# Layer 2's expert blocks: stages two blocks apart with four places between them, and the key numbers loaded ahead of SyncE's fills

## The reference

```
x = hidden_states.reshape(-1, 256)
routing_weights = softmax(x @ gate)                       # 32 experts
top_k_weights, top_k_indices = top_k(routing_weights, 4)
top_k_weights = top_k_weights / top_k_weights.sum(-1)
g, u = split(x @ gate_up_proj[e], 2)                      # 2 x 96 columns
next_states = (u * silu(g)) @ down_proj[e]                # 96 -> 256
out = sum over the 4 chosen experts of weight * next_states
```

## Time and profile before

| | |
|---|---|
| median of 3 runs | 1046.31 us (1046.28 to 1047.95) |
| profiled execution, first to last instruction | 1040.2 us |
| TensorE (weight loads) busy | 862.0 us, 83% (674.7 us, 65%) |
| VectorE, ScalarE, GpSimd busy | 575.4, 359.2, 389.4 us |
| gate/up and down products of the blocks, L742 and L760 | 89.4 and 99.3 us, the latter with layer index 3's |
| scatters of the 95 blocks, L817 | 94.9 us, 999 ns each |
| chain of work that ended last | traced from the end back to 526 us |

### The profile page before, as it was taken

The page is one execution under the profiler, slowest core; times in us unless marked ns, Lnnn a source line. Parts: engine busy times, 40 slices in busy tenths (PEclk is TensorE's granted clock), DMA queues, the critical chain, the costliest instruction groups (busy, mean ns, idle before and its releaser), DMA issues.

```text
span 1040.2 us, 17487 instructions
## 1 busy us (share of the span) xinstructions
PE 862.0 (83%) x5237; PEld 674.7 (65%) x5237; DVE 575.4 (55%) x1679; ACT 359.2 (35%) x1007; POOL 389.4 (37%) x411
## 2 busy tenths in 40 slices
PE   2999998912789899777657898988995998999997
PEld 2787786601667677566546777868553675777786
DVE  5647886550556665628736887943352435444333
ACT  3425242420223333211236777821152323222221
POOL 7210725465345555657534554000046201343100
PEclk9999999965899999978858999995995999999999
DMA  9143205597454444176347776500242201332212
GB/s 352 33 168 75 83 22 185 202 247 191 104 175 131 124 125 142 48 243 226 95 109 163 171 164 154 139 1 1 91 127 82 89 11 58 103 97 83 86 56 107
DMA packets 67244, 126.49 MB, mean 122 GB/s; under 512 B 20004, under 2 KB 49085, under 8 KB 64515
## 3 DMA queue, kind: packets, MB, share of 16 engines
q1 hardware_dynamic: 45407, 74.42, 23.7%
q0 software_dynamic: 20960, 48.76, 16.3%
q10 hardware_dynamic: 788, 2.19, 0.9%
HBM read 87.39 MB, written 43.30 MB: 126 GB/s over the span
## 4 chain that ended last, share of the span: by engine, by line
PE 30%; DMA 8%; DVE 6%; issue 2%; ACT 2%; SPq 2%; POOL 0%; DVEq 0%; POOLq 0%; ACTq 0%
PE ps L460 9%; PE ps L742 5%; PE ps L760 3%; DMA big<-newblk,new_i 2%; PE ps L2396 2%; PE ps L2293 1%; PE ps L2441 1%; PE ps L2335 1%; DMA big<-big 1%; DMA early<-big 1%; DVE work L1861 1%; DVE early L1867 1%; SPq L995 1%; DMA big<-early 1%; PE ps L2397 1%
## 5 line engine op out<-in xcount | busy, mean ns | idle before, releaser
L826 POOL DMA_INDIRECT sent_d<-mid,slot_i x88 | 98.3, 1117 | 117.9 <-DVE mid L621 69.1
L817 POOL DMA_INDIRECT back_d<-early,mid x95 | 94.9, 999 | 90.5 <-DVE early L801 54.1
L760 PE MATMUL ps<-early 96*128 (+1 forms) x346 | 99.3, 387 | 0.7 <-DVE early L795 0.4
L771 ACT ACTIVATE early<-ps 128x256 f32<-128x256 f32 x134 | 51.4, 384 | 133.5 <-PE ps L732 100.7
L788 DVE TENSOR_TENSOR early<-early,ps 128x96 f32<-128x96 f32 (+1 forms) x134 | 37.2, 278 | 106.3 <-ACT early L776 65.9
L742 PE MATMUL ps<-big,early 128*128 x380 | 89.4, 359 | 6.9 <-ACT early L771 3.4
L494 DVE TENSOR_TENSOR hidl<-work,hidh 128x512 fp32r<-128x512 f32 (+1 forms) x56 | 38.7, 691 | 84.4 <-ACT hidh L487 83.7
L817 POOL DMA_INDIRECT back_d<-big,mid x39 | 38.4, 985 | 116.8 <-DVE big L801 114.4
L500 ACT ACTIVATE work<-ps 128x512 f32<-128x512 f32 (+1 forms) x56 | 33.4, 596 | 138.9 <-PE ps L460 136.9
L742 PEld LDWEIGHTS ps<-big,early 128*128 128x128 f32 x380 | 62.1, 197 | 20.9 <-issue 18.2
L732 PE MATMUL ps<-late,mid 128*128 128x128 f32 x268 | 53.2, 281 | 26.7 <-DMA mid<-sent_d,first_i 23.1
(11 more groups left out here) (399 smaller groups left out, 2102.3 us busy)
## 6 DMA issues: line engine op xcount, KB each, us to landing
mid<-sent_d SPq DMA_DIRECT2D x124, 130.0 KB
big<-back_d SPq DMA_DIRECT2D x16, 512.0 KB
early<-back_d SPq DMA_DIRECT2D x16, 256.0 KB, 3.0
early<-in_w SPq DMA_DIRECT2D x3, 1024.0 KB, 11.4
big<-in_gate SPq DMA_DIRECT2D x1, 3072.0 KB, 10.6
big<-in_up SPq DMA_DIRECT2D x1, 3072.0 KB, 15.9
early<-in_gu SPq DMA_DIRECT2D x1, 2816.0 KB, 10.2
sent_d<-work SPq DMA_DIRECT2D x19, 130.0 KB
```

The costliest lines, as they stand in the source:

```text
L760: last = nc.tensor.matmul(ps[:, 6 + j % 2, 0:D], L.hTb[j % 2][0:f1 - f0, h * P:(h + 1) * P], L.down[0:f1 - f0, h, bass.ds(owners[j] * D, D ...
L771: nc.scalar.activation(L.yTb[b % 2], ps[:, b % 2, 0:2 * P], ACT.Copy).then_inc(s["turn_sb"], 1)
L817: nc.gpsimd.indirect_dma_start(out=back_d, out_offset=bass.IndirectOffsetOnAxis(ap=xblk[b % XRING][:, D:D + 1].bitcast(I32), axis=0), in_= ...
L826: nc.gpsimd.indirect_dma_start(out=sent_d, out_offset=bass.IndirectOffsetOnAxis(ap=L.slot_i[:, i:i + 1], axis=0), in_=L.rows[c][:, t, n, : ...
```

## The change

`L1.lag` is 2 and `L3.lag` 1. In turn b TensorE takes T of block b, the gate/up product of block b - lag, the hidden transpose of block b - 2 lag, the down product of block b - 3 lag; ScalarE and VectorE follow. For layer index 1 the loops so have 3 more turns, `yTb`, `hb` and `hTb` have four places (LRING), `sgb`, `ob` and the PSUM banks what they had. Waits for a place to come free now ask for the block four earlier, those for a PSUM bank for the block two earlier, as before. The mask's scratch moves in `early`. On SyncE the wait for `rows_ps` and the load of the key numbers move ahead of the wait for the tables and the fills. Layer index 3 keeps distance 1 and two places.

```diff
+LRING = 4
+L1.lag, L3.lag = 2, 1
...
-        yTb, sgb, hb, hTb, ob = (ring(0, 2, 2 * P), ring(512, 2, F1), ring(704, 2, F1), ring(896, 2, P),
-                                 ring(1152, ORING, D))
+        yTb, sgb, hb, hTb, ob = (ring(0, LRING, 2 * P), ring(1024, 2, F1), ring(1216, LRING, F1), ring(1600, LRING, P),
+                                 ring(2112, ORING, D))
...
-            if 1 <= b <= NB:
-                j = b - 1
+            if lag <= b < NB + lag:
+                j = b - lag
...
-            if 2 <= b <= NB + 1:
-                j = b - 2
+            if 2 * lag <= b < NB + 2 * lag:
+                j = b - 2 * lag
...
-            if b >= 3:
-                j = b - 3
+            if b >= 3 * lag:
+                j = b - 3 * lag
...
+            lag, ring_y = L.lag, len(L.yTb)
             if b < L.NB:
                 act.wait_ge(s["turn_ps"], L.turn0 + b + 1)
-                if b >= 2:
-                    act.wait_ge(s["pair_ps"], L.b0 + b - 1)
-                nc.scalar.activation(L.yTb[b % 2], ps[:, b % 2, 0:2 * P], ACT.Copy).then_inc(s["turn_sb"], 1)
+                if b >= ring_y:
+                    act.wait_ge(s["pair_ps"], L.b0 + b - ring_y + 1)
+                nc.scalar.activation(L.yTb[b % ring_y], ps[:, b % 2, 0:2 * P], ACT.Copy).then_inc(s["turn_sb"], 1)
...
+            sp.wait_ge(s["rows_ps"], NT)
+            k0 = first_at["key"][0]
+            assert first_at["keyless"][0] == k0 + WK
+            sp.dma_start(zm[:, 0:2 * WK], a["first"][:, k0:k0 + 2 * WK]).then_inc(s["keys"], 16)
             sp.wait_ge(s["tables"], AT_FILLS)
             for e in FILLS[0]:
                 r = sp.value_load(L1.endrow_i[0:1, e:e + 1], min_val=e * SPAN1, max_val=e * SPAN1 + T)
                 sp.dma_start(*fill_rows(r, e)).then_inc(s["filled"], 16)
-            sp.wait_ge(s["rows_ps"], NT)
-            k0 = first_at["key"][0]
-            assert first_at["keyless"][0] == k0 + WK
-            sp.dma_start(zm[:, 0:2 * WK], a["first"][:, k0:k0 + 2 * WK]).then_inc(s["keys"], 16)
...
-            for b in range(NBK + 3):
+            for b in range(NBK + 3 * L1.lag):
                 pe_block(pe, L1, b, owners)
```

More of the change, by code:

```diff
@@ L721, in pe_block @@
         def pe_block(pe, L, b, owners):
-            F, NB = L.F, L.NB
+            F, NB, lag = L.F, L.NB, L.lag
             if b < NB:
@@ L751, in pe_block @@
                 for h, (f0, f1) in enumerate(L.parts):
-                    last = nc.tensor.transpose(ps[0:f1 - f0, 4 + j % 2, h * P:(h + 1) * P], L.hb[j % 2][:, f0:f1], ident)
+                    last = nc.tensor.transpose(ps[0:f1 - f0, 4 + j % 2, h * P:(h + 1) * P],
+                                               L.hb[j % len(L.hb)][:, f0:f1], ident)
                 last.then_inc(s["hturn_ps"], 1)
-            if b >= 3:
-                j = b - 3
+            if b >= 3 * lag:
+                j = b - 3 * lag
                 pe.wait_ge(s["hturn_sb"], L.b0 + j + 1)
@@ L759, in pe_block @@
                 for h, (f0, f1) in enumerate(L.parts):
-                    last = nc.tensor.matmul(ps[:, 6 + j % 2, 0:D], L.hTb[j % 2][0:f1 - f0, h * P:(h + 1) * P],
+                    last = nc.tensor.matmul(ps[:, 6 + j % 2, 0:D],
+                                            L.hTb[j % len(L.hTb)][0:f1 - f0, h * P:(h + 1) * P],
                                             L.down[0:f1 - f0, h, bass.ds(owners[j] * D, D)],
@@ L779, in dve_block @@
+            if b >= lag:
+                j = b - lag
+                act.wait_ge(s["pair_ps"], L.b0 + j + 1)
+                if j >= 2:
+                    act.wait_ge(s["prod_sb"], L.b0 + j - 1)
+                nc.scalar.activation(L.sgb[j % 2], ps[:, 2 + j % 2, 0:L.F], ACT.Silu).then_inc(s["act_ready"], 1)
         def dve_block(dve, L, b):
-            F, n = L.F, len(L.parts)
+            F, n, lag = L.F, len(L.parts), L.lag
+            ring_h, ring_t = len(L.hb), len(L.hTb)
             w = L.parts[0][1]
-            if 1 <= b <= L.NB:
-                j = b - 1
+            if lag <= b < L.NB + lag:
+                j = b - lag
@@ L1267, in _ @@
                 act.dma_start(*fill_rows(r, e)).then_inc(s["filled"], 16)
-            for b in range(NBK + 1):
+            for b in range(NBK + L1.lag):
                 act_block(act, L1, b)
@@ L1431, in _ @@
             split_rows(3)
-            for b in range(NB3 + 1):
+            for b in range(NB3 + L3.lag):
                 act_block(act, L3, b)
@@ L2041, in _ @@
             split_rest(3)
-            for b in range(NB3 + 3):
+            for b in range(NB3 + 3 * L3.lag):
                 dve_block(dve, L3, b)
@@ L2481, in _ @@
             owners = {}
-            for b in range(NB3 + 3):
-                if b == 3:
+            for b in range(NB3 + 3 * L3.lag):
+                if b == 3 * L3.lag:
                     pe.wait_ge(s["acc_used"], 3 * NCH + 2)
```

30 lines of the change are left out of this document (12 added, 18 removed).

## The result

The changed kernel took 1035.11 us (median of 4 runs, 1030.98 to 1040.15) against 1047.13 us for the kernel before on the same chip: 0.9868 of it, 95% interval 0.982 to 0.9916. It is faster by 12 us. I had forecast 28.8 us and 1017.5 us, with a range up to 1035.0.

A forecast was written before the change was run, and what follows sets the result against it. Layer 1's expert blocks bound it: a 9.31 us hole at the start, 28.1 us lost to late releases. 431.74 - 402.0 - 0.9 = 28.8 us gained; span 1040.2 - 28.8 = 1011.4, plus 6.1 around it, 1017.5 us; range 1008.5 to 1035.

The forecast's parts named there:

- Key numbers ahead of the fills: Start of layer 1's expert blocks: VectorE's wait for keys goes, block 10's transpose starts at 267.8 instead of 278.15, 10.4 us won.
- The clock: Sign in layer 1's first blocks: TensorE's granted clock at 1.00 by 258.
- Blocks 12 to 17: Loads behind layer 2's weights: stretch stays 11.1 us, longer hole before block 17, block 18 3.36 us later; 10.7 us won so far.
- Stages two blocks apart: Layer 1's loop, blocks 18 to 94: more slack per hand-over cuts 135.96 us to 116.9, 1.54 us a step.
- The floor: Layer 1's loop, blocks 18 to 94: TensorE needs 76 x 1.42 = 107.9 us.
- 28.1 us that I called lost: Same loop: time beyond TensorE's 107.9 us, put down to late releases of results; a third, 9 us, was to stay.
- my 116.9 us: Forecast time of the loop from block 18 to 94: 107.9 + 9 us.
- The slack that I worked out: Layer 1's loop, two blocks apart: 1.4 us for PSUM hand-overs, covering releases 1.0 to 1.4 us late.
- The first rival: Layer 1's loop: late releases are TensorE's true pace, 1.79 us a step is work; 1036.5 us, chance 0.12.
- The tail: After block 94's transpose: seven scatters unsent instead of four, end 11.1 us later instead of 10.2; cost 0.9 us.
- The other rivals: Clock low to block 10 (0.07, 1025 us); GpSimd held by mask steps (0.05, 1024); scatters back late (0.03, 1052.6).
- What surrounds the span: Whole kernel: median taken as 6.1 us above the profiled execution's span, added to 1011.4 for 1017.5 us.

The follow-up runs named there:

- e7: Kernel before with only the key numbers moved ahead of the fills, on a chip where before takes 1052.88 us: 1041.62 us, ratio 0.9894.
- e5: Kernel before, unchanged, run again on the chip where before takes 1052.88 us: 1055.34 us, ratio 1.0018.
- e1: Kernel before with only the key numbers moved ahead of the fills, on a chip where before takes 999.26 us: 996.98 us, ratio 0.997.
- e15: The whole change as it is, on a chip where before takes 995.9 us: 1000.29 us, ratio 1.0038.
- e3: Whole change with layer index 1's experts fixed at build time, no register load, where before takes 999.26 us: 986.9 us, ratio 0.9867.
- e11: Whole change with layer index 1's experts fixed at build time, where before takes 999.95 us: 987.7 us, ratio 0.99.
- e12: Kernel before with keys ahead of the fills and experts fixed at build time, stages one block apart, where before takes 999.95 us: 984.62 us, ratio 0.9882.
- e13: Whole change with layer index 1's experts fixed at build time, where before takes 995.9 us: 987.96 us, ratio 0.9912.
- e6: The whole change as it is, on the chip where before takes 1052.88 us: 1044.03 us, ratio 0.99.
- e8: Whole change with the key numbers back behind the fills, on the chip where before takes 1052.88 us: 1051.25 us, ratio 0.9968.
- e2: Whole change with the key numbers back behind the fills, on the chip where before takes 999.26 us: 1000.14 us, ratio 1.0023.
- e9: Kernel before with keys ahead of the fills and experts read four at a time without range check, stages one block apart: 983.96 us, ratio 0.9852.

## Why the prediction was wrong

**Key numbers ahead of the fills: right.** T10 came at 269.59 for 267.8, 8.6 us earlier than before in place of 10.4, mainly since SyncE's fills began 2.7 us later (226.81 for 224.12). SyncE's block load still decided it. The clock rose at 261, not by 258, and it made no difference, because T10 waited 0.41 us for its data anyway. e7 shows it alone: T0 to T10 21.9 us, 31.8 in e5. The gain belongs to chips with slow fills; e1 shows it as 0.3% within noise.

**Blocks 12 to 17: right.** T17 waited 2.84 us for its load (2.81 before), T18 came 3.08 us later (3.36 before), and T10 to T18 took 17.69 us. I had expected a longer hole; it was of the same length.

**Stages two blocks apart: the step that failed.** It reads "107.9 us that TensorE needs", and "I take a third of today's loss, 9 us of 28.1, as what stays: 107.9 + 9 = 116.9 us". Both halves were off.

The floor was wrong by 9 us. I took it from one step of 1.42 us at 269.03, right after a low clock and a pause. In the loop before, the shortest tenth of the steps is at or below 1.49 us and the median 1.65 us; the median of the undisturbed e15 is 1.52 us. TensorE loads and checks a register in each step, and with it needs 1.54 us (117.0 us in e1 and e15; 107.6 in e3, e11, e12 and e13 without it). Of the 28.1 us that I called lost, 9 were TensorE's own queue. That is shown on the faster kind of chip; on the first chip the same distances between the same instructions stand for it. No distance brings those back: my 116.9 us is, by accident, the pace of a chip with no late result at all.

Of the other 19.0 us (136.0 - 117.0) the distance took back 4.6 us, a quarter, where I had reckoned with two thirds. The slack that I worked out, 1.4 us, was there: TensorE's waits for VectorE went (e5 10.9 us, e6 none among the large rows), and the longest step fell from 3.51 to 2.49 us. But the median step rose from 1.65 to 1.71 us (these three figures are worked out from the starts of the T). The late results are not only late for their readers. TensorE's own queue stands still with them, as the 723 ns wait shows, and "issue" before its weight loads is 14.9 us in the changed loop, 1.5 us in e15. Since that queue fills 1.54 of 1.54 us, each stop in it would be added to the loop; that is argued from these rows, and no run tries it. The ScalarE waits of 43.8 us, on which I rested "such late releases come again and again", were no measure of them: e15 has 39.9 us without one late Y.

The first rival (chance 0.12, 1036.5 us) said in effect that most of this stays, and the time came within 1.4 us of it. Its reason was half right: "1.79 us a step is work" holds for 1.54 of them. Its nearness is in part luck: it had the loop win nothing and the tail lose 0.9 us, and the measured 4.6 and 4.2 us cancel.

That the stops are the cause of the late bunches is seen side by side at two places (309.5 and 316.6) and not tested. A long small instruction is missing at most of the other bunches: of these instructions, loads left out, 6 took over 0.3 us in the changed loop, 12 in e6, 4 in e8, 1 in e5 and none in e7 and in the loop before, while each of them has 21 or more late Y's.

**The tail: mis-sized.** I forecast +0.9 us and it was +4.2. Nine scatters were outstanding at T94, not seven, since GpSimd runs two behind; before, it was six and not four. The three more take 3.8 us. I had set a sum without disturbance against a measured time, in which one scatter waited 1.87 us for VectorE. On the undisturbed chips the distance costs 3.5 us there (12.5 and 9.0 us, e2 and e1).

**The other rivals:** none came. The clock was up from 261, before T10. Scatters have a median of 985 ns as before (984), and in the 76 steps B never waits for one: it does so twice before T18 (1.6 us) and twice in the tail (2.2 us).

**What surrounds the span.** 1.9 us, not 6.1: executions of one kernel spread by 9 us (1031 to 1040 us here) to 17 us (988 to 1005 us in e1), and I had taken the distance from one execution to the median as a constant. By terms the sum would then have been 1040.2 + 1.9 - 28.8 = 1013.3 us, further off. The range missed by 0.1 us because it was cut short of the rival's value.

## What to carry to other kernels

Before one gives an engine more distance, ask what its own step costs without any wait, from many steps and not from the fastest one, and count its register loads, checks and waits beside its arithmetic, by the distances between their starts: a TensorE "busy" for 100% of a loop (e15) still had 8% in it that its matmuls did not need. Grouping four register loads into one, without their range checks and with the keys ahead, took 0.985 to 0.9925 of before in three runs, where on the same kind of chip the keys alone took 0.997 and the whole change 1.0038. It made the distance pointless there. A deeper pipeline pays its depth again at the end, here 3.5 us, and the transfer that is late in one chip's trace can be early on another.

## What the runs showed of the hardware

I had not expected two kinds of chips. The same kernel takes 996 to 1000 us on four and 1047 to 1053 us on two. The granted clock in the loop is about the same, 0.99. What differs is that small instructions of SyncE and TensorE now and then take some 0.7 us on the two, and that a part of the semaphore events is missing in their traces (above). It shows in these rows, the fills of e15 and of e5:

```profile
218.28 28.05 SPq L969 DMA_DIRECT2D sent_d<-work  x18
```

```profile
224.47 38.85 SPq L957 DMA_DIRECT2D sent_d<-work  x18
```

and in the loop, where a step takes 1.54 us without a late result, or 1.73 to 1.88 us with one in about every four steps. The version of e9 was run on no chip of the slower kind, so what it brings there isn't known.

A register load on TensorE with its arithmetic and check shows 0.47 us and costs 0.66 us when the queue is full. Twelve waits written one behind the other on one semaphore became six instructions of 51 ns a step, 106 ns from start to start.
